# Attention's output projection as f32r products of parts, one step later, with the input and the keys' rows in one slot each

## The reference, cut to what matters

```python
P = (X @ W_in + b_in).reshape(b, t, HEADS, 256)          # 16 heads: Q, K, V, G of 64 each
W = jnp.power(EPS + _cdist(Q, K), -2)
W = W / (EPS + jnp.sum(W, axis=-1, keepdims=True))
H = G * jnp.einsum('hbts,hbse->hbte', W, V)
H = jnp.transpose(H, (1, 2, 0, 3)).reshape(b, t, 1024)
x = x + H @ W_out + b_out                                # the projection that is changed
x = x + experts(layernorm(x))                            # 8 experts, top 2 of a softmax
```

## Time and profile before

| | |
|---|---|
| median of the three runs | 1420.71 us |
| profiled execution: device time, span in the trace | 1424.09 us, 1422.3 us |
| mean granted clock of TensorE | 0.995 |
| busy: PE, DVE, ACT, POOL | 1386.1, 1096.4, 1099.9, 835.2 us |
| output projection (line 451) on PE | 128 matmuls shown, 60.3 us busy |
| POOL: sums of weights (lines 317, 320), multiplication (line 326) | 158.9, 317.6, 76.4 us |

### The profile page before, as it was taken

How to read it: one execution, slowest core, us unless ns; L and a number is a source line. 1 busy time by engine, 2 the same in 40 slices (tenths; PEclk the granted TensorE clock), 3 DMA queues, 4 the chain that set the end, 5 groups by cost and what they waited for, 6 DMA issues and landing times.

```text
span 1422.3 us, 18183 instructions
## 1 busy us (share of the span) xinstructions
PE 1386.1 (97%) x6496; PEld 744.1 (52%) x6496; DVE 1096.4 (77%) x1995; ACT 1099.9 (77%) x947; POOL 835.2 (59%) x655
## 2 busy tenths in 40 slices
PE   8999999999999999999999999899999999999995
PEld 5444444444444444444444444445777777777774
DVE  7887897788888887887888788635677686786757
ACT  2799889969978978979979979945676776776751
POOL 4568777778778778768867876411333333333330
PEclk9999999999999999999999999999999999999999
DMA  3000010011101101101101012343011010110100
GB/s 113 1 17 17 24 46 17 23 27 36 24 16 46 24 16 39 30 17 31 38 16 32 17 30 68 108 142 106 1 68 60 8 68 2 67 60 9 68 1 15
DMA packets 45705, 54.99 MB, mean 39 GB/s; under 512 B 13808, under 2 KB 32368, under 8 KB 44464
## 3 DMA queue, kind: packets, MB, share of 16 engines
q1 hardware_dynamic: 45616, 53.84, 12.7%
HBM read 48.97 MB, written 4.85 MB: 38 GB/s over the span
## 4 chain that ended last, share of the span: by engine, by line
PE 86%; DVE 8%; ACT 5%; issue 1%; DMA 0%; DVEq 0%; SPq 0%
PE sc L406 14%; PE av L419 13%; PE z L74 12%; PE pj L74 12%; PE y L1191 8%; PE sc L401 6%; PE y L74 5%; PE pj L383 4%; PE pj L451 4%; DVE w L597 3%; PE pj L429 2%; ACT w L684 1%; ACT w L688 1%; ACT w L680 1%; DVE high L565 1%
## 5 line engine op out<-in xcount | busy, mean ns | idle before, releaser
L597 DVE TENSOR_SCALAR w<-sc 128x1024 f32<-128x1024 f32 x256 | 301.2, 1217 | 69.4 <-PE sc L406 67.3
L680 ACT ACTIVATE w<-w 128x2048 f32<-128x2048 f32 x128 | 237.6, 1904 | 123.3 <-DVE w L597 123.0
L320 POOL TENSOR_TENSOR wsum<-wsum,w 128x512 f32<-128x512 f32 x248 | 317.6, 1281 | 19.4
L963 POOL TENSOR_TENSOR hr_l<-hr,hr_h 128x512 fp32r<-128x512 f32 x112 | 149.9, 1338 | 263.0 <-ACT hr L1013 263.0
L406 PE MATMUL sc<-query,key 64*128 64x512 f32 x1024 | 243.3, 594 | 0.0
L684 ACT ACTIVATE w<-w 128x2048 f32<-128x2048 f32 x128 | 240.1, 1899 | 0.4
L688 ACT ACTIVATE w<-w 128x2048 f32<-128x2048 f32 x128 | 239.8, 1897 | 0.0
L419 PE MATMUL av<-w,vt 128*64 128x512 f32 x1024 | 233.8, 598 | 2.6 <-ACT w L688 2.5
L1013 ACT ACTIVATE hr<-z,b 128x512 f32<-128x512 f32 x256 | 173.6, 685 | 67.8 <-PE z L74 67.7
L306 POOL TENSOR_TENSOR sqq<-query 128x512 f32<-128x512 f32 x63 | 65.5, 1040 | 187.1 <-DVE query L537 153.0
L317 POOL TENSOR_TENSOR wsum<-w 128x512 f32<-128x512 f32 x124 | 158.9, 1282 | 5.2 <-ACT w L688 5.2
(11 more groups left out here) (213 smaller groups left out, 2360.5 us busy)
## 6 DMA issues: line engine op xcount, KB each, us to landing
hT<-head_recips SPq DMA_DIRECT2D x64, 256.0 KB, 4.0
rb<-routing SPq DMA_DIRECT2D x8, 2048.0 KB, 7.1
w<-in_W SPq DMA_DIRECT2D x16, 256.0 KB, 5.1
xa<-in_X SPq DMA_DIRECT2D x8, 256.0 KB, 4.5
xc<-in_X SPq DMA_DIRECT2D x8, 256.0 KB, 2.8
x<-xc SPq DMA_DIRECT2D x8, 256.0 KB, 4.0
x<-x SPq DMA_DIRECT2D x1, 1792.0 KB, 8.1
out<-prod SPq DMA_DIRECT2D x7, 256.0 KB, 2.3
```

Source lines behind the costliest of these rows:

```text
L320: nc.gpsimd.tensor_tensor(wsum[:, u, :], wsum[:, u, :], w[:, j % 2, u, c, :], ALU.add).then_inc(s_added, 1)
L597: nc.vector.tensor_scalar(w[:, s, 2 * r:2 * r + 2, c, :], sc[:, i, :, :], 0.0, None, ALU.max).then_inc(s_d2, 1)
L680: nc.scalar.activation(w[:, j % 2, u, :, :], w[:, j % 2, u, :, :], ACT.Sqrt).then_inc(s_sqrt, 1)
```

## The change

The output projection becomes a product of parts. ACT makes the high part of `wout` once, in front of the powers of step 1, and POOL the low part. For each quad ACT makes the high part of `hT` (between the second and the third square root of a step), POOL the low part (between the third and fourth group of adds). The projection runs one step later (quad j-4), the turning of the output and its adding and storing move from q = 2 to q = 3, and POOL's multiplication is written at the end of an iteration instead of at the start of the next, which is the same place in POOL's order. `xs` and `krow` get one slot each; the new tiles lie partly over others that are done (`until_split`). For the last three quads POOL makes both parts (`last_parts`). At the end of the attention the outputs 28 to 31, the last reciprocals and the last turned output stand later among the expert products, the second weights are split later (by DVE over the end of the first and the start of the second batch), the routing weights `rb0` are loaded in two pieces, and batch 6 is stored in SP's program of the rest.

The diff, cut to its core:

```diff
-        xs = [sb("xh", [P, 2, T], F32R), sb("xl", [P, 2, T], F32R)]
+        xs = [sb("xh", [P, T], F32R), sb("xl", [P, T], F32R)]
...
-        krow = sb("krow", [P, 2, 2, T], F32R)
+        krow = sb("krow", [P, 2, T], F32R)
...
-        wout = sb("wout", [P, PAIRS, D])
+        wout_h = sb("wout_h", [P, PAIRS, D], F32R)
+        with ExitStack() as until_split:
+            wout_f = until_split.enter_context(nc.sbuf_tensor("wout", [P, PAIRS, D], F32))
+        wout = [wout_h, sb("wout_l", [P, PAIRS, D], F32R)]
...
-        hT = sb("hT", [P, 2, 2, T])
+        with ExitStack() as until_split:
+            hT = until_split.enter_context(nc.sbuf_tensor("hT", [P, 2, 2, T], F32))
+        hT_l = sb("hT_l", [P, 2, 2, T], F32R)
+        hT_h = sb("hT_h", [P, 2, T], F32R)
...
-            if k == 1 and 0 <= j - 3 < NQ:
-                names.append(("out", j - 3))
-            if k == 2 and q == 2 and b >= 1:
+            if k == 1 and 0 <= j - 4 < NQ:
+                names.append(("out", j - 4))
+            if k == 2 and q == 3 and b >= 1:
                 names.append(("out_t", b - 1))
...
-                if q == 0 and b >= 1:
+                if q == 1 and b >= 1:
                     store_x1(b - 1)
                     load_x(xc, b, s_xc)
...
+            def low_part(j):
+                pool.wait_ge(s_hT_h, j + 1)
+                nc.gpsimd.tensor_tensor(hT_l[:, j % 2, :, :], hT[:, j % 2, :, :], hT_h[:, :, :].bitcast(F32),
+                                        ALU.subtract).then_inc(s_hT_l, 1)
+            def last_parts(j):
+                pool.wait_ge(s_hT, j + 1)
+                pool.wait_ge(s_pj, use["out", j - 1] + 1)
+                nc.gpsimd.tensor_copy(hT_h[:, :, :], hT[:, j % 2, :, :]).then_inc(s_hT_h, 1)
+                low_part(j)
             for j in range(-1, NQ):
-                if 0 <= j - 3 < NQ:
-                    normalize(j - 3)
...
-                if 0 <= j - 1 < NQ:
-                    for u in range(4):
+                if j == 1:
+                    pool.wait_ge(s_wout, 1)
+                    nc.gpsimd.tensor_tensor(wout[1][:, :, :], wout_f[:, :, :], wout[0][:, :, :].bitcast(F32),
+                                            ALU.subtract).then_inc(s_wout, 1)
+                for u in range(4):
+                    if 0 <= j - 1 < NQ:
                         add_chunks(j - 1, u)
-            return normalize
+                    if u == 2 and 0 <= j - 3 < NQ:
+                        low_part(j - 3)
+                if 0 <= j - 2 < NQ:
+                    normalize(j - 2)
+            return normalize, last_parts
...
-                if j == NQ - 3:
-                    fill(nc, pj[:, n, :], ident, 4)
-                pe.wait_ge(s_hT, j + 1)
+                if j == NQ - 4:
+                    fill(nc, pj[:, n, :], ident, 2)
+                pe.wait_ge(s_hT_l, j + 1)
                 for r in range(2):
-                    m = nc.tensor.matmul(pj[:, n, :], wout[:, 2 * (j % QUADS) + r, :], hT[:, j % 2, r, :],
-                                         start=(r == 0), stop=(r == 1))
+                    m = product(nc, pj[:, n, :], [w[:, 2 * (j % QUADS) + r, :] for w in wout],
+                                [hT_h[:, r, :], hT_l[:, j % 2, r, :]], start=(r == 0), stop=(r == 1))
...
+            def high_part(j):
+                act.wait_ge(s_hT, j + 1)
+                if j >= 1:
+                    act.wait_ge(s_pj, use["out", j - 1] + 1)
+                nc.scalar.copy(hT_h[:, :, :], hT[:, j % 2, :, :]).then_inc(s_hT_h, 1)
             def square_roots(j):
                 for u in range(4):
                     r, v = divmod(u, 2)
+                    if u == 2 and j >= 3:
+                        high_part(j - 3)
                     act.wait_ge(s_d2, 8 * j + 4 * r + 4)
...
             for j in range(NQ - 1):
+                if j == 1:
+                    act.wait_ge(s_late_in, 16 * N_LATE)
+                    nc.scalar.copy(wout[0][:, :, :], wout_f[:, :, :]).then_inc(s_wout, 1)
                 weights(j)
...
-            normalize = att_gpsimd(pool)
-            normalize(NQ - 3)
+            normalize, last_parts = att_gpsimd(pool)
+            last_parts(NQ - 3)
             normalize(NQ - 2)
+            last_parts(NQ - 2)
             normalize(NQ - 1)
+            last_parts(NQ - 1)
...
-                if (b, k) == (0, 7):
+                if (b, k) == (0, 4):
+                    output(NQ - 3)
+                if (b, k) == (0, 10):
                     output(NQ - 2)
-                if (b, k) == (0, 16):
+                if (b, k) == (0, 19):
                     output(NQ - 1)
-                if (b, k) == (0, 18):
+                if (b, k) == (0, 22):
                     turn_output(B - 1)
...
-                if n == NU + 1:
-                    pe.wait_ge(S["w2s"], NE * NF)
+                if b == 1 and i == 1:
+                    pe.wait_ge(S["w2s"], NF * (k // NF + 1))
...
-                if (b, k) == (0, 20):
+                if (b, k) == (0, 22):
                     output(NQ - 1)
-                if (b, k) == (0, 21):
+                if (b, k) == (0, 24):
                     add_output(B - 1)
-                if b == 0 and k >= 24:
+                if 28 <= n < 28 + NE:
```

More of the change, by code:

```diff
@@ L187, in build_attention @@
         s_hT = sem("s_hT")
+        s_hT_h = sem("s_hT_h")
+        s_hT_l = sem("s_hT_l")
+        s_wout = sem("s_wout")
         s_xc = sem("s_xc")
@@ L191, in build_attention @@
         N_LATE = 3
-        PERIODS = range(-1, NQ + 3)
+        PERIODS = range(-1, NQ + 4)
         SLOTS = 4
@@ L363, in values @@
                     pe.wait_ge(s_rest_l, 2)
-                product(nc, pj[:, bank(("v", b, n)), :], [x[:, b % 2, c * P:(c + 1) * P] for x in xs],
+                product(nc, pj[:, bank(("v", b, n)), :], [x[:, c * P:(c + 1) * P] for x in xs],
                         [v[:, h * T:(h + 1) * T] for v in wv]).then_inc(s_pj, 1)
@@ L373, in projection @@
                 product(nc, pj[:, bank(("p", j, i)), :], [m[:, 2 * q + i // 3, i % 3, :] for m in wqkg],
-                        [x[:, b % 2, :] for x in xs]).then_inc(s_pj, 1)
+                        [x[:, :] for x in xs]).then_inc(s_pj, 1)
             def squared_lengths(j, name, squares):
@@ L400, in distances @@
                     for v in range(2):
-                        nc.tensor.matmul(sc[:, i, v, :], krow[halves[v], j % 2, g % 2, c * P:(c + 1) * P],
+                        nc.tensor.matmul(sc[:, i, v, :], krow[halves[v], g % 2, c * P:(c + 1) * P],
                                          qrow[halves[v], j % 2, :], start=True, stop=False)
@@ L475, in step @@
                         values(b, n)
-                if k == 1 and 0 <= j - 3 < NQ:
-                    output(j - 3)
-                if k == 2 and q == 2 and b >= 1:
+                if k == 1 and 0 <= j - 4 < NQ:
+                    output(j - 4)
+                if k == 2 and q == 3 and b >= 1:
                     turn_output(b - 1)
@@ L585, in key_rows @@
                     dve.wait_ge(s_high, 4 * j + 2 * r + 2)
-                    nc.vector.scalar_tensor_tensor(krow[:, j % 2, r, :], source, row[:, r, 3:4], high[:, :].bitcast(F32),
+                    nc.vector.scalar_tensor_tensor(krow[:, r, :], source, row[:, r, 3:4], high[:, :].bitcast(F32),
                                                    ALU.mult, ALU.subtract).then_inc((s_high, s_pj_free)[r], 1)
@@ L918, in spread_routing @@
                     sp.wait_ge(att["gated"], 2 * (NQ - 1))
-                sp.dma_start(rb[f % 2][:, :, :], rwd[f % 2].partition_broadcast(P)).then_inc(S["rb"], 16)
+                    sp.dma_start(rb0[:, 0:NE - 2, :], rwd[0, 0:NE - 2].partition_broadcast(P)).then_inc(S["rb"], 16)
+                else:
+                    sp.dma_start(rb[f % 2][:, :, :], rwd[f % 2].partition_broadcast(P)).then_inc(S["rb"], 16)
             def store(t):
@@ L1263, in _ @@
             sums(NQ - 2)
-            output(NQ - 3)
+            output(NQ - 4)
             turn_f(0)
@@ L1529, in step @@
                     sums(NQ - 1)
+                if (b, k) == (0, 5):
+                    output(NQ - 3)
+                if (b, k) == (0, 4):
                     for e in range(5, NE):
```

42 lines of the change are left out of this document (24 added, 18 removed).

## The result

The changed kernel takes **1434.8 us** (median of 6 runs, 1434.2 to 1436.6) against 1421.8 us (6 runs, 1420.4 to 1423.5): 1.0091 times as long, 95% interval 1.008 to 1.0102. The forecast was 1422.7 with a range to 1428, so the direction given the highest chance came true by a thin margin (slower 0.41, no change 0.39), and the size lies outside the range: 13 us instead of 2. The profiled execution took 1434.75 us, span 1433.0 against 1422.3. The two traces thus show 10.7 of the 13.0 us; the rest is that the traced execution of the kernel before, 1424.09 us, was itself 2.3 above the median of its runs.

The account below looks back on a forecast made before the run. PE was taken to bound the attention loop, but not the hand-over. -7.9 + 4.0 + 5.5 + 0.4 = +2.0 us on the profiled 1424.09 gave 1426.1, or 1422.7 for the median (3.4 lower); range 1415 to 1428.

Parts of the forecast that it names:

- PE, per step: Attention steps with an output: projection takes 1.48 us on PE instead of 1.80, 0.32 us less.
- One-slot tiles: Input's parts and keys' rows in one slot each: cost nothing, since DVE's order hides them.
- ACT, per step: High part's copy, 1.05 us, falls into ACT's 1.43 us wait for DVE: costed at nothing.
- POOL's loop: Attention steps: low part makes POOL's loop 26.0 us; q = 3 becomes 26.11, q = 2 falls only 0.56.
- The loop, A: Sum over all attention steps of what PE gains and POOL limits: -7.9 us.
- The start, B: First head sums wait for W_out's low part on POOL, then half clock: +4.0 us, bounds 2.4 and 4.4.
- The hand-over, C: Attention to experts: POOL's last adds wait for ACT's copy and the low part: +5.5 us, bounds 1.0 and 8.
- ACT had 1.84 us to spare: Hand-over: slack for the routing's logits, taken off the 5.5 us delay, so 3.7 at least moves through.
- Later, D: Among the experts: moved outputs, a new 1.4 us routing-weights wait, smaller turning waits: +0.4 us, bounds -1.0 and +2.0.
- The first, waits covered: Rival, chance 0.22: waits at start and hand-over covered or small, B 2.4 and C 1.0, giving 1416.6 us.
- The second, the low part outgrowing its room: Rival, chance 0.16: in q = 2 and 3, POOL's low part takes 3.0 us: 1430, half of it 1426.
- The third: Rival, chance 0.10: PE's clock falls at the hand-over too, behind 5 us of idle: +1.7, 1424.5 us.

Follow-up runs that it names:

- e12: Kernel before the change, with one slot used for the input's parts and the keys' rows: 1423.5 us against 1422.7 beside it.
- e11: Changed kernel with POOL's low part halved to 128x512 for outputs 0 to 27, PE doing the same work: 1428.9 us.
- e8: Changed kernel, but POOL makes copy and low part of output 29 only after DVE has made the first expert's weight parts: 1432.3 us.
- e3: Changed kernel, but in the last step ACT makes output 28's high part in front of the first square roots: 1429.2 us.
- e4: Changed kernel with 34 instead of 10 filling matmuls on PE in front of the last-but-one head sums: 1433.4 us.
- e9: Changed kernel with the edits of e1, e3, e5, e6 and e8 together: 1418.9 us, 0.9975 of the kernel before the change.
- e6: Changed kernel with the last output and last turning, and their additions on DVE, moved to earlier expert chunks: 1432.9 us.
- e5: Changed kernel, but POOL makes copy and low part of output 31 only after DVE has normalized the next batch's input: 1431.3 us.
- e10: As e9, with POOL's output 28 low part and output 29 multiplication after DVE's first expert normalization, and output 28 behind the routing's logits: 1419.6 us.
- e2: Changed kernel, but in the last step POOL makes output 28's low part behind all four groups of adds: 1429.8 us.
- e7: Changed kernel with the low parts of outputs 0 to 28 made by DVE instead of POOL: 1440.1 us.
- e1: Changed kernel, but POOL makes W_out's low part behind the sixteen adds of its iteration 1 instead of in front: 1431.9 us.

## Why the prediction was wrong, step by step

- **PE, per step: right.** 1.48 us instead of 1.80, as worked out. The 0.231 us of a product held; the Trainium skill's figure (TensorE: Matmul & The Clock Gate, Back-to-back issue gap) of 0.216 us would have given 1.39 and was rightly set aside.
- **One-slot tiles: right** (e12). **ACT, per step: right**: the copy took 1.03 us, and ACT still waits for DVE behind it, 1.07 us in q = 3 and 0.26 in q = 0.
- **POOL's loop: right mechanism.** q = 2 came to 27.1 us (27.0 expected), bound by POOL (e11); q = 3 to 26.18 (26.11), bound by PE.
- **The loop, A = -7.9: measured -6.1.** Seven steps each of q = 0 and 1 gave 0.28 us instead of 0.32, six of q = 2 gave 0.43 instead of 0.56, six of q = 3 cost 0.19 instead of 0.12: 0.6 + 0.8 + 0.4 us. Sizes, not a cause.
- **The start, B = +4.0: measured +3.3** (2.6 at the first head sums, 0.8 in the two steps behind; within the bounds). The first head sums were due at 77.8 to 77.9 and came at 77.73, with the half clock.
- **The hand-over, C = +5.5: measured +9.7. This is the step that failed.** The wait was found: the adds ended 5.5 us later against ACT's chain (+2.7 with ACT at -2.8), exactly as worked out. What was put behind it was wrong in two ways. First, "ACT had 1.84 us to spare" was taken for the slack of the whole hand-over. It is that of the logits alone; PE's own chain, with the experts' input and the first weights' parts, had 0.79 us in the kernel before:

```profile
915.67 3.65 PE L419 MATMUL av<-w,vt 128*64 128x512 f32 x16 [0.79 <-ACT w L688]
```

  Second, DVE held up by POOL (2.0 us at the cast, e8) and the clock (half speed in the head sums and output 28, partly in av, +1.6 us there, gone in e8) were left in the bounds or in a rival of 0.10, as if they were other cases. Neither is another case. The clock fell behind the 3.80 us of idle that the wait itself makes. The hold-up does not even need the wait: in e3, without it, the cast still took 1.98 us beside the low part of output 29, which is new work in every case. From the adds' end to the first expert product it took 11.6 us instead of 8.1: 2.0 of the 3.4 us are the cast (e8), of the rest e4's fills gave back 0.9. The terms that the traces show are then 5.5 less 0.79 of slack, plus 3.4, plus 1.6 in av: 9.7. With the wait and the hold-up gone (e9) the hand-over costs 1.0 us, ACT's copy alone: the lower bound given.
- **Later, D = +0.4: measured +3.8.** The DMAs, output 29 and the new wait for the routing weights (1.91 us, 1.4 expected, in place of the old 1.42, e6) were near. The failing part is "less 0.4 of PE's smaller waits for the next batch's turning": that wait grew from 0.96 to 3.80. The copy and low part of output 31 follow the multiplication that already lay beside DVE's normalization; the earlier trace rows showed what one POOL operation does to it, and I did not ask which DVE work the new two would meet (e5). With e5 and e6, D is +0.85 (e9).
- **Rivals.** The first, waits covered, is what e9 had to build by hand. The second, the low part outgrowing its room, did not happen: 32 of them took 2.34 to 2.69 us. The third was no rival but a part of the forecast's own case.
- **The sum**, in the two traces: 3.3 - 6.1 + 9.7 + 3.8 = 10.7 against 4.0 - 7.9 + 5.5 + 0.4 = 2.0. Of the 8.7 us missed, 4.2 are the hand-over's and 3.4 are Later's.

## What to carry to other kernels

Before work is added to an engine that shares access with another, list every operation of the other that it will lie beside outside the steady loop: a gain of 0.2 us a step on average was lost at three places that occur once. When a wait is found at a hand-over, price what follows from it (the clock after the idle, the neighbour's work that comes to lie beside it) in the same sum, and take the slack from the chain that ends last, not from the one that is easiest to read. Here one reordered copy and a few waits on the cheap engine turned the change from 0.9% slower into 0.25% faster.

## What the runs showed of the hardware

- **DVE's casts, scalings and subtractions between SBUF tiles got through only in gaps of POOL's operations.** Four scalings of 0.34 us took 1.1 us with POOL idle (e10), 2.9 beside one POOL operation, 5.9 beside three and 8.05 beside four in a row (e2). The one that adds an output of PE from PSUM kept its length, 0.65 to 0.75 us, in all traces. e7 shows that it works both ways: whoever starts first goes through. By the Trainium skill (SBUF — State Buffer, SBUF: two separate sides) the two share a pair of ports under a lock that the earlier instruction holds to its end, and the other blocks fully, for operations of these kinds; these rows agree.
- **POOL's copy with rounding is quick:** 1.04 us for 128x1024, against 2.38 for the subtraction of two tiles of that size. I had taken 2.1.
- **The same idle does not always cost the clock.** Behind PE's wait of 3.80 us at 967 the changed kernel kept the full clock; in e1, behind 3.88 us at 962, the clock of the stretch was 0.87 and two chunks took 1.91 us instead of 1.02. Windows of 962 to 975 us, the changed kernel and then e1:

```profile
962.00:975.00 13.00, 9.20 (x38) 5.90 (x37) 8.66 (x12) 5.40 (x9) 4.54 (x3) 1.00 0.01 1
```

```profile
962.00:975.00 13.00, 12.56 (x44) 8.29 (x45) 4.14 (x11) 5.54 (x8) 0.04 (x1) 0.87 0.00 1
```

  It cost e1 1.65 us of its lead. In e6 and e8 the clock fell there too (0.87 and 0.74 in these windows), in e4 and e5 only behind the next wait. The trace of the change kept it at both places. Why one falls and the other doesn't was not tried; it may also be behind the two groups of times in e5.
